# A routed two-pass expert kernel: how GpSimd's row gathers are spread over the pairs of tiles

## The chip, the cores and the metric

One core of one Trainium2 chip runs the kernel. The metric is the time of one execution in device microseconds; the time given is a median of several executions. A separate, profiled execution gives the trace.

## The reference, cut to what matters

```python
x = x + 0.5 * ffn(layernorm(x))        # pass 0
x = x + attention(layernorm(x))
x = x + 0.5 * ffn(layernorm(x))        # pass 1

def ffn(x):                            # x: 2048 tokens x 256
    scores = softmax(x @ gate_weight.T)            # 32 experts in 8 groups
    ... the best 3 groups, of those the best 6 experts for each token, weights normalised
    for e in range(32):                            # I = 128
        h = silu(x @ w1[e].T) * (x @ w3[e].T)
        y += combine[:, e, None] * (h @ w2[e].T)
    return y + silu(x @ sw1.T) * (x @ sw3.T) @ sw2.T      # the shared expert
```

Everything is float32. The attention between the two is a chunked linear attention over 16 heads; the change does not touch it.

## The kernel before, in words

The feed-forward part runs twice, as `moe(0)` and `moe(1)` (pass 0 and pass 1, `f` in the code). It does not compute every expert for every token. It sorts the 12288 choices (2048 tokens x 6) by expert, 96 full blocks of 128 rows, and cuts them into tiles of 128 rows that belong to one expert each. There are at most 128 such tiles, worked on in `NQ` = 64 pairs. The gathered rows make `NP` = 48 pairs of blocks; the last 16 pairs of tiles need no new rows.

The work of one pair q goes through the engines like this:

- GpSimd gathers the token rows of two blocks from a table in HBM by an indirect DMA (L399), into one of `RX` = 8 row buffers.
- TensorE transposes them two pairs ahead (`transpose_in`, L901, counts `e_xp`), VectorE copies them to a ring (L680, counts `e_in`), ScalarE picks the tile's columns (L492, `e_xt`).
- TensorE multiplies with w1 and w3 (`up`, L911, counts `e_h`), ScalarE takes the SiLU (`gate`, L469, `e_s`), VectorE multiplies (L690, `e_g`), TensorE transposes (L923), VectorE copies (L697), TensorE multiplies with w2 (`down`, L931), ScalarE copies the result out (`output`, L477, `e_y`), and SP stores two pairs at a time to a table of slots in HBM (L322), counting stored tiles in `s_there`.

ScalarE works in laps of `RA` = 4 pairs and reads register values for the ring columns at the start of each lap (L481). Every engine runs its instructions in the order written; engines meet only at semaphores.

When a column of results is there, its rows come back: GpSimd gathers, for the 16 blocks of tokens and for one of the six choices at a time ("column" n), the result rows from the table (L420), and VectorE adds them to x, weighted (`add_row`, L730). Pass 0 returns 2 columns this way (32 gathers, `returned` has 20 buffers), and leaves the other four columns to the attention part (L195). Pass 1 returns all six (96 gathers, `KEEP` = 28 buffers). Gather number g, counted over the columns, waits for `stored` (the tiles of that column are in the table), for a free buffer (`s_add`), and in pass 0 for `e_h`.

VectorE's last eight pairs (56 to 63) have four adds each: column 0 in pairs 56 to 59, column 1 in pairs 60 to 63 (L751 to L753). An add of a column waits until all 16 gathers of that column have landed (L721). These adds stand between the copy of one pair and the multiply of the next.

Behind pair 63 of pass 1, SP loads the tokens again (L353), TensorE computes the shared expert in four parts (L817, L830), and VectorE's order is fixed: adds of column 2, `product(0)` (L579), adds of column 3, `product(1)`, two shared additions (L669), adds of column 4, `product(2)`, shared additions, `product(3)`, adds of column 5 in two halves. TensorE's part n waits for `product(n - 1)`. In pass 0 the attention follows instead.

GpSimd's gathers of token rows wait on `e_xp`. With `AHEAD` = 4 and `EDGE` = 8, pass 0 lets pair q start once pair q - 4 has been transposed for q from 4 to 19, and once pair q - 8 has been from q = 20 on; pass 1 uses a lead of 4 for q from 4 to 11 and of 8 from q = 12 on.

Of the kernel before, what the change touches and what calls it, by code (L numbers as in the profile page):

```python
# [16 lines left out]
NT = T // P  # L17
# [11 lines left out]
NQ = ST // 2  # L29
# [7 lines left out]
RX = 8  # L37
EDGE = 8
AHEAD = 4
FILLS, FILL = 6, 8  # L40
EARLY = 2
REST = TOPK - EARLY
RY = 2
RA = 2 * RY
KEEP = 28
RO = 4
# [24 lines left out]
def begun(value):  # L71

    return not isinstance(value, int) or value > 0
# [7 lines left out]
def hold(eng, sem, value, held):  # L81

    eng.wait_ge(sem, value)
    eng.sem_inc(held, 1)
# [23 lines left out]
def program(nc, x_in, w13_in, w2_in, gate_in, sw13_in, sw2_in, wqkv_in, wg1_in, wg2_in, wo_in, nw_in,  # L110
            const_in, turn_in, out, table, y_table, columns_table):
    ctx = ExitStack()
    with ctx:
# [3 lines left out]
        def sem(name):  # L117
            return ctx.enter_context(nc.semaphore(name))
# [13 lines left out]
        def c(name, a=0, b=None):  # L132
# [5 lines left out]
        s_held, s_half, s_fill, s_again = sem("s_held"), sem("s_half"), sem("s_fill"), sem("s_again")  # L138
        s_rows, s_yst = [sem(f"s_rows{u}") for u in range(RX)], [sem(f"s_yst{u}") for u in range(RY)]
        e_xp, e_in, e_xt, e_h, e_s, e_g, e_gp, e_gt, e_yp, e_y = (  # L140
            sem(f"e_{n}") for n in ("xp", "in", "xt", "h", "s", "g", "gp", "gt", "yp", "y"))
# [21 lines left out]
        def inverse_root(chp, out, value, ready):  # L163

            chp(nc.gpsimd.tensor_tensor(out, value, eps_ln[:, :], ALU.add))
            nc.gpsimd.tensor_tensor(out, out, half[:, :], ALU.pow).then_inc(ready, 1)
# [37 lines left out]
        def moe(f, combine, share, ring, area, sw13, sw2):  # L204
# [7 lines left out]
            with ExitStack() as mem:  # L212
                def sb(name, shape, dt=F32):
                    return mem.enter_context(nc.sbuf_tensor(f"{name}_{f}", shape, dt))
# [24 lines left out]
                else:  # L239
                    y = [sb(f"ey{u}", [P, 4 * H]) for u in range(RY)]  # L240
                    s1, gTs = w13[:, 0:KS * TB], [w13[:, (u + 1) * KS * TB:(u + 2) * KS * TB] for u in range(2)]
# [39 lines left out]
                done, read = f * NQ, f * NP  # L281

                def v3(ap, k):
                    return ap.rearrange("p (t k) -> p t k", k=k)
# [11 lines left out]
                with nc.Block() as block:  # L296
                    @block.sync
                    def _(sp):
# [20 lines left out]
                        def store(it, u):  # L319
                            m = it * RY + u  # L320
                            sp.wait_ge(e_y, done + m * 2 + 2)
                            sp.dma_start(y_table.rearrange("(p t) h -> p t h", t=ST)[:, bass.ds(m * 4, 4), :],  # L322
                                         y[u].rearrange("p (t h) -> p t h", h=H)).then_inc(s_yst[u], 16)
                            if f == 1 or u > 0:
                                sp.wait_ge(s_yst[(u - 1) % RY], (it + f * (NQ // 2 // RY) + (u > 0)) * 16)
                            else:
                                sp.wait_ge(s_yst[(u - 1) % RY], it * 16)
                            sp.sem_inc(s_there, 4)  # L328
# [33 lines left out]
                    @block.gpsimd  # L362
                    def _(pool):
                        if f == 0:
                            nc.gpsimd.memset(half[:, :], -0.5).then_inc(s_half, 1)
                            chp(nc.gpsimd.memset(eps_ln[:, :], LN_EPS))

                        def sentinels():

                            for k in range(NG - TOPG):  # L370
                                value = -3.1e38 - 5e36 * k
                                nc.gpsimd.memset(low[:, k:k + 1], value)
                                last = nc.gpsimd.memset(v3(group, PADG)[:, :, NG + k:NG + k + 1], value)
                                if k < PADE - E:
                                    last = nc.gpsimd.memset(v3(val, PADE)[:, :, E + k:E + k + 1], value)
                            nc.gpsimd.memset(ones[:, :], 1.0)
                            nc.gpsimd.memset(most[:, :], 0.0)
                            nc.gpsimd.memset(ones16[:, :], 1.0).then_inc(s_low, 1)

                        if f == 0:  # L380
                            sentinels()
                        for k in range(NT // 2):
                            pool.wait_ge(s_var, 2 * k + 2)
                            inverse_root(chp, rs[:, 2 * k:2 * k + 2], v3(mv[:, :], 2)[:, 2 * k:2 * k + 2, 1], s_rstd)
                            if f == 1 and k == 1:
                                sentinels()

                        pool.wait_ge(s_st, 80)
                        pool.wait_ge(s_slots, 1)
                        for q in range(NP):  # L390
                            if f == 0 and AHEAD <= q < EDGE + RX + AHEAD:
                                pool.wait_ge(e_xp, q - AHEAD - max(0, q - EDGE - AHEAD) // EDGE + 1)
                            elif AHEAD <= q < EDGE + AHEAD:
                                pool.wait_ge(e_xp, read + q - AHEAD + 1)
                            elif q >= RX:
                                pool.wait_ge(e_xp, read + q - RX + 1)
                            for a in range(2):
                                t = 2 * q + a
                                pool.indirect_dma_start(  # L399
                                    out=rows[q % RX][:, a * H:(a + 1) * H], out_offset=None, in_=table,  # L400
                                    in_offset=bass.IndirectOffsetOnAxis(ap=slots[:, t:t + 1], axis=0)
                                ).then_inc(s_rows[q % RX], 16)

                        def stored(k):

                            end = pool.value_load(last_of_column[k:k + 1, 0:1], min_val=1, max_val=ST)
                            hold(pool, s_there, end + 4, s_held)

                        pool.wait_ge(s_known, 2)
                        pool.wait_ge(e_xp, read + NP)  # L410
                        for n in range(columns):
                            k = TOPK - 1 - n
                            stored(k)
                            for i in range(NT):
                                g = n * NT + i
                                if g >= len(returned):
                                    pool.wait_ge(s_add, g - len(returned) + 1)
                                if f == 0 and g % 2 == 0:
                                    pool.wait_ge(e_h, NQ - NT - 3 + g // 2)
                                pool.indirect_dma_start(  # L420
                                    out=returned[g % len(returned)], out_offset=None, in_=y_table,
                                    in_offset=bass.IndirectOffsetOnAxis(
                                        ap=combine[:, i * TOPK + k:i * TOPK + k + 1], axis=0)
                                ).then_inc(s_back[n] if n < TOPK - 1 else s_last[i // 4], 16)

                    @block.scalar
                    def _(act):
# [43 lines left out]
                        def output(q, u, lap):  # L471

                            act.wait_ge(e_yp, done + q + 1)
                            stored = (f * (NQ // RA) + lap) * 16
                            if u % 2 == 0 and begun(stored):
                                act.wait_ge(s_yst[u // 2], stored)
                            nc.scalar.copy(y[u // 2][:, u % 2 * 2 * H:(u % 2 + 1) * 2 * H], bY[u % 2][:, :]).then_inc(e_y, 1)  # L477
# [17 lines left out]

                        def pairs(q0, lap, n=RA, first=False, more=True):

                            column = columns_of(q0 * 2 + 2, 2 * n if more else 2 * n - 2)
                            for i in range(n):
                                if i < n - 1 or more:  # L500
                                    tile_columns(q0 + i + 1, i + 1, column[2 * i:2 * i + 2])
                                gate(q0 + i, i)
                                if i > 1 or not first:
                                    output(q0 + i - 2, (i - 2) % RA, lap - (i < 2))

                        act.wait_ge(s_known, 1)
                        tile_columns(0, 0, columns_of(0, 2))
                        pairs(0, 0, first=True)
                        with act.Fori(0, NQ // RA - 2) as it:
                            pairs(it * RA + RA, it + 1)  # L510
                        pairs(NQ - RA, NQ // RA - 1, more=False)
                        for u in range(2):
# [1190 lines left out]
```

## Time and profile before

| | |
|---|---|
| median of 3 executions | 966.11 us (962.2 to 973.23) |
| profiled execution | 960.5 us |
| its span, first to last instruction | 958.7 us |
| mean granted TensorE clock | 0.893 |
| GpSimd gathers of token rows (L399) | 192, mean 973 ns, 186.7 us busy |
| GpSimd gathers of returned rows (L420) | 124 + 4, mean 1049 ns |
| bytes moved by DMA | 126.43 MB, mean 132 GB/s |

In the rows of the next section, times are in microseconds from the start of the span unless marked ns. A line of the timeline gives start, duration, engine, source line, operation, what is written and read, how often, and in brackets how long the engine was idle before and what ended that. "x4" is four instructions merged. The trace names the source lines of the kernel above. Multiplies of VectorE (L690) can be counted: there are 64 in each pass, and multiply q is the one of pair q, counted from 0.

### The profile page before, as it was taken

To read this page: it belongs to the slowest core of one execution; us is meant where nothing else is said; L and a number is where in the kernel's file an instruction comes from. 1 tells how busy PE (TensorE), PEld (TensorE's weight loads), DVE (VectorE), ACT (ScalarE), POOL (GpSimd) and SP (SyncE) were. 2 spreads that over 40 slices of the span, in tenths; PEclk is the share of its full clock that TensorE was granted. 3 is DMA by queue.
4 is the path that set the end of the run, shared out by engine and by line. 5 is a ranking of instruction groups with operands and counts; after the bars stand their busy time and mean duration, and the time that the engine had idled before them with its cause. 6 is when DMAs were issued, how large, how long until landed. Compare 5 with 4: busy or idle time off the path is not lost. (4 is left out here: it accounts for less than half of the span.)

```text
span 958.7 us, 16120 instructions
## 1 busy us (share of the span) xinstructions
PE 772.8 (81%) x4554; PEld 609.0 (64%) x4555; DVE 513.0 (54%) x1439; ACT 358.5 (37%) x799; POOL 465.3 (49%) x487
## 2 busy tenths in 40 slices
PE   6895997999969789788889575686999995867486
PEld 6464885888847546576677374564888884645154
DVE  5774942434313537888887469672444431135274
ACT  3160443444424314465665224233444442322000
POOL 3005665553053335867754320655555406456884
PEclk9979898999988898999999755688999998887798
DMA  6862465643233463222220140233444413334524
GB/s 209 338 286 77 158 214 176 231 164 120 89 121 114 159 227 89 80 76 67 72 62 2 34 176 1 77 121 120 153 158 154 138 77 121 126 112 131 207 82 153
DMA packets 42358, 126.43 MB, mean 132 GB/s; under 512 B 8352, under 2 KB 16704, under 8 KB 39488
## 3 DMA queue, kind: packets, MB, share of 16 engines
q1 hardware_dynamic: 23872, 75.40, 20.7%
q0 software_dynamic: 18432, 50.36, 18.0%
q8 instruction: 29, 0.48, 0.2%
q14 instruction: 25, 0.20, 0.1%
HBM read 76.44 MB, written 49.28 MB: 131 GB/s over the span
## 5 line engine op out<-in xcount | busy, mean ns | idle before, releaser
L399 POOL DMA_INDIRECT back<-token_table,slots x192 | 186.7, 973 | 221.9 <-DVE slots L644 96.3
L911 PE MATMUL bank<-w,xt 128*128 x1024 | 260.7, 400 | 33.2 <-ACT xt L492 18.4
L911 PEld LDWEIGHTS bank<-w,xt 128*128 128x128 f32 x1024 | 196.5, 200 | 69.4 <-issue 44.2
L420 POOL DMA_INDIRECT back<-slot_table,combine x124 | 130.0, 1049 | 143.6 <-SPq L328 42.2
L690 DVE TENSOR_TENSOR mids<-mids,bank 128x256 f32<-128x256 f32 x128 | 53.8, 420 | 256.6 <-ACT mids L469 197.3
L931 PE MATMUL bank<-w,mids 128*128 x512 | 142.9, 405 | 4.5 <-DVE mids L697 2.6
L492 ACT COPY xt<-ring 128x256 f32 x256 | 91.5, 408 | 104.0 <-issue 75.9
L931 PEld LDWEIGHTS bank<-w,mids 128*128 128x128 f32 x512 | 93.2, 203 | 16.0 <-issue 7.1
L469 ACT ACTIVATE mids<-bank 128x256 f32<-128x256 f32 x128 | 49.0, 383 | 145.2 <-PE bank L911 87.8
L680 DVE COPY ring<-bank 128x512 f32 (+1 forms) x96 | 66.1, 689 | 46.6 <-PE bank L901 31.2
L923 PE MATMUL bank<-const,mids 128*128 128x128 f32 x256 | 52.6, 290 | 45.7 <-DVE mids L690 24.2
L195 POOL DMA_INDIRECT ring<-slot_table,combine x64 | 64.4, 1006 | 34.9 <-issue 17.4
L923 PEld LDWEIGHTS bank<-const,mids 128*128 128x128 f32 x256 | 36.7, 148 | 63.3 <-issue 29.4
L901 PE MATMUL bank<-const,back 128*128 128x128 f32 x384 | 60.9, 284 | 3.2 <-DMA back<-token_table,slots 3.2
L1111 POOL TENSOR_TENSOR root_a<-power_a,half 128x17 f32<-128x17 f32 (+2 forms) x20 | 51.3, 2564 | 21.1 <-DVE power_a L1465 13.0
L901 PEld LDWEIGHTS bank<-const,back 128*128 128x128 f32 x384 | 50.1, 147 | 14.3 <-DMA back<-token_table,slots 3.4
L477 ACT COPY ey<-bank 128x512 f32<-128x512 f32 x64 | 37.4, 584 | 54.7 <-PE bank L931 31.2
L697 DVE COPY mids<-bank 128x256 f32<-128x256 f32 x128 | 53.4, 417 | 5.7 <-PE bank L923 3.2
L477 ACT COPY gT<-bank 128x512 f32<-128x512 f32 x64 | 37.4, 585 | 49.9 <-PE bank L931 38.3
L730 DVE SCALAR_TENSOR_TENSOR x<-back,share,x 128x256 f32<-128x256 f32 x124 | 50.7, 477 | 4.1 <-DMA back<-slot_table,combine 3.9
L1483 DVE SCALAR_TENSOR_TENSOR ring<-bank,own_a 128x512 f32<-128x512 f32 x64 | 39.7, 683 | 14.4 <-remote 9.6
L817 PE MATMUL bank<-w,sw 128*128 128x512 f32 x64 | 32.0, 659 | 16.9 <-DMA w<-token_columns 12.3
(209 smaller groups left out, 1070.9 us busy)
## 6 DMA issues: line engine op xcount, KB each, us to landing
slot_table<-gT SPq DMA_DIRECT2D x32, 512.0 KB
slot_table<-ey SPq DMA_DIRECT2D x32, 512.0 KB
w<-in_w SPq DMA_DIRECT2D x12, 1024.0 KB, 17.1
slot_table<-w SPq DMA_DIRECT2D x6, 1024.0 KB
token_table<-back SPq DMA_DIRECT2D x8, 512.0 KB, 2.9
back<-token_table,slots POOLq DMA_INDIRECT x192
x<-in_x SPq DMA_DIRECT2D x4, 512.0 KB, 5.7
turn_a<-in_turn SPq DMA_DIRECT2D x4, 512.0 KB
```

The source lines that it names most:

```text
L195: nc.gpsimd.indirect_dma_start(out=back[j % RB][:, k * H:(k + 1) * H], out_offset=None, in_=y_table, in_offset=bass.IndirectOffsetOnAxis(a ...
L399: pool.indirect_dma_start(out=rows[q % RX][:, a * H:(a + 1) * H], out_offset=None, in_=table, in_offset=bass.IndirectOffsetOnAxis(ap=slots ...
L420: pool.indirect_dma_start(out=returned[g % len(returned)], out_offset=None, in_=y_table, in_offset=bass.IndirectOffsetOnAxis(ap=combine[:, ...
L477: nc.scalar.copy(y[u // 2][:, u % 2 * 2 * H:(u % 2 + 1) * 2 * H], bY[u % 2][:, :]).then_inc(e_y, 1)
L492: last = nc.scalar.copy(xt[u % 2][:, a * H:(a + 1) * H].rearrange("p (k i) -> p k i", k=KC), blocks[:, :, bass.ds(column[a], P)])
L680: last = nc.vector.tensor_copy(blocks[:, :, bass.ds(at, 2 * P)].rearrange("p k (a i) -> p k a i", a=2), new)
L690: nc.vector.tensor_tensor(two(eg[u % 2][:, :]), two(es[u % 2][:, :]), part(u, 1), ALU.mult).then_inc(e_g, 1)
L697: nc.vector.tensor_copy(egT[u % 2][:, :], bG[u % 2][:, 0:2 * P]).then_inc(e_gt, 1)
L901: last = nc.tensor.transpose(bX[u % 2][:, a * H + k * P:a * H + (k + 1) * P], rows[u][:, a * H + k * P:a * H + (k + 1) * P], ident)
L911: last = nc.tensor.matmul(bH[u % 2][:, a * 2 * I:(a + 1) * 2 * I], xt[u % 2][:, a * H + k * P:a * H + (k + 1) * P], w13[:, bass.ds(expert[ ...
L923: last = nc.tensor.transpose(bG[u % 2][:, a * P:(a + 1) * P], eg[u % 2][:, a * I:(a + 1) * I], ident)
L931: last = nc.tensor.matmul(bY[u % 2][:, a * H:(a + 1) * H], egT[u % 2][:, a * I:(a + 1) * I], w2[:, bass.ds(expert[a] * H, H)], start=True, ...
```

## The change

The wait ahead of the gathers of token rows becomes one rule for both passes: from pair 4 on, pair q waits until pair q - 4 of the same pass has been transposed. `read` is 0 in pass 0 and 48 in pass 1.

The wait ahead of the returned rows changes its numbers and now holds for both passes. With `done` 0 in pass 0 and 64 in pass 1, every second gather waits until `e_h` has reached 48 + g/2 in pass 0 (before: 45 + g/2), and 47 + g/2 in pass 1 (before: no such wait), as long as that number is at most 64. That is all 32 gathers in pass 0 and g up to 35 in pass 1. `e_h` counts finished up-products, so `e_h` = n means that up-product n - 1 is done. Nothing else is changed.

```diff
@@ constants
 RY = 2
+PACED = NQ - NT, NQ - NT - 1
 RA = 2 * RY
@@ GpSimd, gathers of token rows
                         for q in range(NP):
-                            if f == 0 and AHEAD <= q < EDGE + RX + AHEAD:
-                                pool.wait_ge(e_xp, q - AHEAD - max(0, q - EDGE - AHEAD) // EDGE + 1)
-                            elif AHEAD <= q < EDGE + AHEAD:
+                            if q >= AHEAD:
                                 pool.wait_ge(e_xp, read + q - AHEAD + 1)
-                            elif q >= RX:
-                                pool.wait_ge(e_xp, read + q - RX + 1)
                             for a in range(2):
@@ GpSimd, gathers of returned rows
                                 if g >= len(returned):
                                     pool.wait_ge(s_add, g - len(returned) + 1)
-                                if f == 0 and g % 2 == 0:
-                                    pool.wait_ge(e_h, NQ - NT - 3 + g // 2)
+                                if g % 2 == 0 and PACED[f] + g // 2 <= NQ:
+                                    pool.wait_ge(e_h, done + PACED[f] + g // 2)
                                 pool.indirect_dma_start(
```

## Rows read from the trace of the kernel before

**Rows 1.** The page, busy time, share of the span and instructions of each engine.
```profile
PE 772.8 (81%) x4554; PEld 609.0 (64%) x4555; DVE 513.0 (54%) x1439; ACT 358.5 (37%) x799; POOL 465.3 (49%) x487
```
**Rows 2.** Waits of ScalarE: who waited for whom, us in total, times, longest us.
```profile
ACT mids L469 <- remote: 54.8, 9, 8.7
...
ACT ey L477 <- remote: 14.9, 4, 8.1
...
ACT gT L477 <- remote: 6.7, 1, 6.7
```
**Rows 3.** The chain of work that ended last, around 650 us: start, us, what.
```profile
649.13 7.92 another core or an unknown queue
```
**Rows 4.** Timeline of VectorE, twelve multiplies of pairs 13 to 63, pass 0 then pass 1.
```profile
139.76 0.42 DVE L690 TENSOR_TENSOR mids<-mids,bank 128x256 f32<-128x256 f32 x1 [0.83 <-issue]
...
160.65 0.42 DVE L690 TENSOR_TENSOR mids<-mids,bank 128x256 f32<-128x256 f32 x1 [3.21 <-ACT mids L469]
...
176.73 0.42 DVE L690 TENSOR_TENSOR mids<-mids,bank 128x256 f32<-128x256 f32 x1 [0.82 <-issue]
...
188.22 0.42 DVE L690 TENSOR_TENSOR mids<-mids,bank 128x256 f32<-128x256 f32 x1 [2.98 <-ACT mids L469]
...
256.49 0.42 DVE L690 TENSOR_TENSOR mids<-mids,bank 128x256 f32<-128x256 f32 x1 [2.92 <-ACT mids L469]
...
264.29 0.42 DVE L690 TENSOR_TENSOR mids<-mids,bank 128x256 f32<-128x256 f32 x1 [2.06 <-ACT mids L469]
...
269.23 0.42 DVE L690 TENSOR_TENSOR mids<-mids,bank 128x256 f32<-128x256 f32 x1 [4.18 <-ACT mids L469]
...
334.24 0.42 DVE L690 TENSOR_TENSOR mids<-mids,bank 128x256 f32<-128x256 f32 x1 [0.47 <-ACT mids L469]
...
641.30 0.41 DVE L690 TENSOR_TENSOR mids<-mids,bank 128x256 f32<-128x256 f32 x1
...
662.70 0.42 DVE L690 TENSOR_TENSOR mids<-mids,bank 128x256 f32<-128x256 f32 x1 [3.79 <-issue]
...
793.70 0.42 DVE L690 TENSOR_TENSOR mids<-mids,bank 128x256 f32<-128x256 f32 x1 [2.06 <-ACT mids L469]
...
883.68 0.41 DVE L690 TENSOR_TENSOR mids<-mids,bank 128x256 f32<-128x256 f32 x1
```
**Rows 5.** Stretches: bounds, length, GpSimd busy (x instructions), clock, DMA share, GB/s.
```profile
137.00:152.00 15.00, 11.37 (x12) 0.93 0.63 211
176.00:191.00 15.00, 7.92 (x9) 1.00 0.61 216
267.00:284.50 17.50, 13.27 (x14) 0.86 0.48 147
...
637.50:656.00 18.50, 14.04 (x14) 0.97 0.42 131
```
**Rows 6.** Timeline of ScalarE, the copy out ahead of gate 15, pass 0.
```profile
154.24 0.59 ACT L477 COPY gT<-bank 128x512 f32<-128x512 f32 x1 [6.72 <-remote]
```
**Rows 7.** Timeline, the last gather of column 1 in pass 0 and its add.
```profile
324.03 1.19 POOL L420 DMA_INDIRECT back<-slot_table,combine  x1 [0.30 <-DVE x L730]
...
327.25 1.67 DVE L730 SCALAR_TENSOR_TENSOR x<-s,share,x 128x256 f32<-128x256 f32 x4 [1.67 <-DMA back<-slot_table,combine]
```
**Rows 8.** Stretches, line L420 alone; columns as in rows 5.
```profile
790.00:875.60 85.60, 47.77 (x50) 0.84 0.40 129
...
882.85:948.50 65.65, 52.47 (x44) 0.84 0.42 134
```
**Rows 9.** Timeline, the tail of pass 1: VectorE, gather 79, TensorE's weight load.
```profile
910.40 1.28 DVE L579 TENSOR_TENSOR w<-w,bank 128x512 f32<-128x512 f32 x2 [17.72 <-issue]
...
924.20 0.96 POOL L420 DMA_INDIRECT back<-slot_table,combine  x1 [0.30 <-issue]
...
927.03 6.42 DVE L730 SCALAR_TENSOR_TENSOR x<-back,share,x 128x256 f32<-128x256 f32 x16 [3.91 <-DMA back<-slot_table,combine]
...
934.70 0.40 PEld L817 LDWEIGHTS bank<-w,sw 128*128 128x128 f32 x2 [2.39 <-DVE w L579]
```

## The prediction

> **What bounds the kernel now.** I read the busy times first [rows 1]: TensorE is busy 81% of the span and GpSimd half of it, so the end is set by TensorE's pace and by what stops it. Then I read the waits [rows 2]. ScalarE waits for something the profile cannot name ("remote") 14 times in three groups, 76.4 us together, at most 8.7 us at once. The chain that ended last runs through such a wait [rows 3], so they are on the path: ScalarE hands the gate to VectorE, VectorE to TensorE, and all three stand.
>
> The pace is read from VectorE's multiply, one for each pair of tiles. Three pairs with the start of a ScalarE lap in them take 11.49 us (176.73 to 188.22) while TensorE also transposes gathered rows, and a whole lap of four takes 12.74 us (256.49 to 269.23) once it does not, 4.94 of it at the lap's start (264.29 to 269.23) and 7.8 in the other three pairs [rows 4].
>
> Last I asked what GpSimd does at the stalls [rows 5]. Where it issues gathers back to back (12 from 137 us, 14 from 267 us, 14 from 637.5 us), a ScalarE stall of 7 to 8 us falls inside or just behind. Where it issues two for each pair (9 in 15 us from 176 us), there is none, and the pace holds. The stalls also sit at different pairs of the two passes, though both run the same ScalarE loop: before pair 15 in pass 0 [rows 6], before pair 7 in pass 1 [rows 3]. I read this as: a row of eight or more gathers without a pause holds ScalarE up for about 7 us.
>
> **The change, part by part.**
>
> *Lead of four pairs throughout.* Before, pair 20 of pass 0 and pair 12 of pass 1 are where the wait falls back from four pairs to eight, and GpSimd issues four extra pairs at once. The change removes both bursts. Pass 0: multiply 13 to multiply 16 took 20.89 us (139.76 to 160.65), the same stretch of a later lap 11.49 [rows 4]: 9.4 us saved. Pass 1: multiply 5 to 8 took 21.40 us (641.30 to 662.70) against 11.49: 9.9 us saved. Cost: every gather now starts only four pairs ahead. Two take 2.2 to 2.5 us on GpSimd, and the last lands 2.0 us behind its end (325.22 to 327.25) [rows 7], against four pairs of lead, some 13 us; pass 0 already ran pairs 4 to 19 on it. I take nothing; if that cover went, TensorE's transposes would wait, and with 5 us of slack lost each lap this would be a large cost. The first bursts (75 us and 604 us) have the same waits as before and stay.
>
> *Returned rows, pass 0.* Before, gathers g and g+1 go once up-product 44 + g/2 is done (counted from 0), which let 14 leave in a row. Now it is up-product 47 + g/2. The first two start as before, since there the wait on the stores decides. Multiply 47 to 63 took 69.95 us (264.29 to 334.24). At the pace it is 4.94 + 3 x 12.74 + 7.8 = 51.0, so 19.0 go. A new wait comes: VectorE adds the second column's rows from pair 60 on and needs all 16. The last two now wait for up-product 62, which by the pace of 2.6 us ends about 4.8 us after multiply 60. Two gathers (2.2 to 2.5) and the landing (2.0) make 9.0 to 9.3, four adds (1.66) 10.7 to 11.0, where multiply 61 was due at 2.6. Queued behind the adds on VectorE are multiply 61 and the copy for TensorE, which stands meanwhile. About 1 us comes back, as up-product 62 is already done, and 1 goes to the lower clock that such pauses brought before. That is 8.1 to 8.4 us; I take 8.5, with bounds 0 (hidden) and 13. Net 10.5 saved.
>
> *Returned rows, pass 1.* Multiply 47 to 63 took 89.98 us (793.70 to 883.68), 39.0 above 51.0. The last two gathers of the second column wait for up-product 61, one pair earlier, so the same wait is 8.5 - 2.6 = 5.9; I take 5.5, bounds 0 and 10. Net 33.5 saved.
>
> *The tail of pass 1.* This is what the pacing costs. When up-product 63 ended (875.6 us), 50 of the 96 gathers had been issued [rows 8]; now it will be 34. The other 62 go back to back at 1.265 us each (0.96 and a gap of 0.30 [rows 9]). Let M be multiply 63. The gather that closes the fifth column (number 79) ended at M + 41.5 before (924.20 + 0.96). Now it ends at M - 0.2 + 46 x 1.265 = M + 58.0, or M + 64.6 if the slow gathers of the old tail recur (52.47 us busy for 44, where 44 x 0.96 is 42.2). VectorE already waited 3.91 us for that column, and product 2 and TensorE's last shared product follow it directly [rows 9]. So the lateness counts in full: +16.5 to +23, and +26 with the lower clock in TensorE's longer waits. I take +20. The columns before it are covered: the third lands by M + 20 to 24.5, and its 16 adds (6.4 us) are done about when product 0 is due (M + 26.7, 910.40). SP's stores and loads are not moved; the waits on stored rows are met before the new ones.
>
> Sum: -9.4 - 9.9 - 10.5 - 33.5 + 20 = -43.3 us. The profiled execution took 960.5 us (span 958.7), so it would take 917; the median of the runs shown lies 5.6 above it, and I predict **922 us** for the median.
>
> A rule that speaks against this: the Trainium skill (SBUF — State Buffer, Who interferes with whom) says that TensorE and ScalarE never wait on another engine at SBUF. By it no gather could hold ScalarE there and the sum would be rival A's. The rows show coincidence in every burst, not the path by which it acts; I go by the rows.
>
> **Rivals.**
>
> *A. The stalls belong to ScalarE's own stream, not to the gathers (slower).* The place is ScalarE's wait ahead of the gate and the output copy. For it: "remote" names no engine. Against: the different pairs in the two passes, and none in the steady stretch. Price: nothing saved, column waits 8.5 + 5.5, tail +20: 960.5 + 34 = 994, as a median 1000. It decides once less than 34 of the 77 us above the pace (9.4 + 9.9 + 19.0 + 39.0) go away. The Trainium skill (Runtime: NRT & Kernel Launch, Instruction fetch mechanics) has a mechanism for it: a taken branch to code outside the fetched pages stops an engine until a DMA has brought it. By that rule the time would be this rival's. No row here ties a stall to one.
>
> *B. Half the gain.* Two gathers for each pair, beside stores and adds, still provoke two or three stalls of 7.9 us between pairs 48 and 63: +16 to +24, so 938 to 946. For it: the old trace had most of its stalls there. Against: the pace holds with two for each pair elsewhere.
>
> *C. A wash.* The stalls get shorter instead of going: half of 77 saved, costs 34, so 956, as a median 961.
>
> *D. More.* The column waits are hidden and the tail stays at 16.5: 77.3 - 16.5 = 60.8 saved, 905 or less.
>
> **How the numbers follow.** The forecast has 0.62, with its own range 905 to 938 (column waits 0 to 13 and 0 to 10, tail 16.5 to 26). B has 0.17, A 0.09, C and D 0.06 each. The range 903 to 950 takes in the forecast, B and some of D. One per cent, 9.7 us, is about what a measurement of this kernel can tell from no change. Faster by more: forecast, B and D, 0.85. Same: C, 0.06. Slower: A, 0.09.
>
> **What would show it.** Right: no "remote" wait of ScalarE above 3 us around multiply 15 of pass 0 and multiply 7 of pass 1; returned gathers in twos about 3 us apart; VectorE waiting 5 us or more for a returned row at pair 60 of both passes; 34 returned gathers at up-product 63 of pass 1; the last shared product 65 to 75 us behind multiply 63, not 51. Wrong: ScalarE stalls of 7 us with gathers in twos (A or B), or an end later than 101 us behind multiply 63 (75.0 before).

## The result and the profile after

The changed kernel took 926.6 us (median of 4, 919.38 to 927.35) against 964.91 us (median of 4, 962.2 to 973.23). The ratio is 0.957, 95% interval 0.950 to 0.965: faster by 4.3%. The profiled execution took 926.16 us, 34.3 us less than the 960.5 us before.

The changed code is three lines shorter, so L466 is now ScalarE's gate, L474 its output copy, L687 the multiply, L727 the add of returned rows, L417 the gather of returned rows, L576 and L814 the product and TensorE's shared products. The waits first (who waited for whom, us in total, times, longest us):

```profile
DVE x L727 <- DMA back<-slot_table,combine: 64.0, 5, 17.0
...
ACT mids L466 <- remote: 11.7, 3, 7.5
```

ScalarE's "remote" waits are down from 14 with 76.4 us [rows 2] to 3 with 11.7 us at the gate, and one more of 2.1 us in the attention (L1334); the one of 7.5 us is that of the very first row of gathers, which the change leaves alone. VectorE now waits 64.0 us for returned rows.

**Who is late in a "remote" wait.** The profile writes "remote" where a semaphore rises and no instruction that raises it ended in the 1.5 us before. It does not mean that nobody is known to raise it. Here is the stall of pair 7 of pass 1 in the kernel before: the up-product of TensorE, the gate of ScalarE that waits for it, TensorE's next matmuls, and the gather of GpSimd that waits for TensorE's transposes:

```profile
649.37 1.99 PE L911 MATMUL bank<-w,xt 128*128 x8 [1.67 <-issue]
...
657.08 0.38 ACT L469 ACTIVATE mids<-bank 128x256 f32<-128x256 f32 x1 [7.95 <-remote]
...
658.04 0.69 PE L923 MATMUL bank<-const,mids 128*128 128x128 f32 x2 [6.69 <-DVE mids L690]
...
658.15 0.96 POOL L399 DMA_INDIRECT back<-token_table,slots  x1 [2.38 <-remote]
```

The up-product ends at 651.36 in the profile, where the ends of matmuls are modelled. Its count `e_h` rises at 657.05 in the trace's semaphore records, 5.7 us later, and the gate starts at once. All 31 "remote" waits of this trace, 14 of ScalarE, 10 of VectorE and 7 of GpSimd, are waits for a count that TensorE raises, and so are the 223 in the nine other traces below that have any. The results of ScalarE and VectorE came on time: in the 128 pairs of this trace the multiply, the transposes and the down-product start at most 0.15 us after what they wait for and their own engine are ready, while the gate starts up to 8.2 us after. So ScalarE is not what is held: TensorE's results, or its word of them, come late, and whoever needs them waits. Whether the matmuls themselves ran long or only their counts were late is not shown. "ScalarE stalls" in the texts below is to be read in this way.

What GpSimd does in the stretches that had rows of 12 and 14 gathers (bounds, length, busy and instructions, clock, DMA share, GB/s):

```profile
137.00:152.00 15.00, 8.44 (x9) 1.00 0.61 220
176.00:191.00 15.00, 8.51 (x9) 1.00 0.50 173
```

The stretch from 137 us has the same nine gathers as the quiet one, and TensorE's granted clock is 1.00 in it; before it was 12 gathers at 0.93 [rows 5]. The multiplies of pairs 16, 47 and 63 of pass 0, then 5, 47 and 63 of pass 1, answer to [rows 4]:

```profile
151.25 0.42 DVE L687 TENSOR_TENSOR mids<-mids,bank 128x256 f32<-128x256 f32 x1 [2.78 <-ACT mids L466]
...
254.84 0.42 DVE L687 TENSOR_TENSOR mids<-mids,bank 128x256 f32<-128x256 f32 x1 [2.06 <-ACT mids L466]
...
318.14 0.42 DVE L687 TENSOR_TENSOR mids<-mids,bank 128x256 f32<-128x256 f32 x1 [1.70 <-ACT mids L466]
...
627.41 0.41 DVE L687 TENSOR_TENSOR mids<-mids,bank 128x256 f32<-128x256 f32 x1
...
769.02 0.42 DVE L687 TENSOR_TENSOR mids<-mids,bank 128x256 f32<-128x256 f32 x1 [2.06 <-ACT mids L466]
...
826.92 0.42 DVE L687 TENSOR_TENSOR mids<-mids,bank 128x256 f32<-128x256 f32 x1 [1.50 <-ACT mids L466]
```

Multiply 47 to 63 takes 63.3 us in pass 0 (69.95 before) and 57.9 us in pass 1 (89.98 before). The waits that took the stalls' place are the adds of column 1 at pair 60 (one line for each pass) and, in the tail, those of columns 3 and 4, the last followed by TensorE's last shared product:

```profile
310.28 1.67 DVE L727 SCALAR_TENSOR_TENSOR x<-s,share,x 128x256 f32<-128x256 f32 x4 [12.06 <-DMA back<-slot_table,combine]
...
819.21 0.92 DVE L727 SCALAR_TENSOR_TENSOR x<-back,share,x 128x256 f32<-128x256 f32 x2 [7.31 <-DMA back<-slot_table,combine]
...
869.54 6.42 DVE L727 SCALAR_TENSOR_TENSOR x<-back,share,x 128x256 f32<-128x256 f32 x16 [13.47 <-DMA back<-slot_table,combine]
...
892.56 6.42 DVE L727 SCALAR_TENSOR_TENSOR x<-back,share,x 128x256 f32<-128x256 f32 x16 [14.21 <-DMA back<-slot_table,combine]
...
900.23 0.50 PEld L814 LDWEIGHTS bank<-w,sw 128*128 128x128 f32 x2 [11.37 <-DVE w L576]
```

The gathers of returned rows of pass 1, ahead of the last multiply and behind it (L417 alone), answer to [rows 8]:

```profile
760.00:826.50 66.50, 32.84 (x34) 0.95 0.42 138
826.50:924.00 97.50, 67.89 (x62) 0.79 0.43 138
```

34 before and 62 behind, as counted ahead of time. Behind the last pair GpSimd issues almost without a pause. TensorE waits for products there, and its granted clock is 0.79 on average, against 0.84 in the tail before [rows 8].

### The profile page after: what moved, and what is told of

It is laid out like the page before. It is cut to its first block and busy times, and to the rows that moved or that the text cites. A ratio compares the mean times of both kernels' runs of the same rounds, so it can differ in the third digit from the quotient of the medians.

```text
span 924.4 us, 16124 instructions
## 1 busy us (share of the span) xinstructions
PE 761.2 (82%) x4554; PEld 602.4 (65%) x4555; DVE 512.7 (55%) x1439; ACT 359.2 (39%) x799; POOL 462.8 (50%) x487
## 3 DMA queue, kind: packets, MB, share of 16 engines
q1 hardware_dynamic: 23872, 75.40, 21.4%
## 5 line engine op out<-in xcount | busy, mean ns | idle before, releaser
L908 PE MATMUL bank<-w,xt 128*128 x1024 | 251.7, 390 | 16.5 <-ACT xt L489 12.3
L908 PEld LDWEIGHTS bank<-w,xt 128*128 128x128 f32 x1024 | 191.0, 195 | 49.0 <-issue 25.9
L417 POOL DMA_INDIRECT back<-slot_table,combine x124 | 127.9, 1031 | 101.8 <-PE bank L908 64.0
L687 DVE TENSOR_TENSOR mids<-mids,bank 128x256 f32<-128x256 f32 x128 | 53.7, 420 | 193.1 <-ACT mids L466 143.3
L928 PE MATMUL bank<-w,mids 128*128 x512 | 135.5, 388 | 1.6 <-DVE mids L694 1.6
L928 PEld LDWEIGHTS bank<-w,mids 128*128 128x128 f32 x512 | 88.9, 194 | 10.6 <-issue 3.2
L466 ACT ACTIVATE mids<-bank 128x256 f32<-128x256 f32 x128 | 48.8, 381 | 93.5 <-PE bank L908 76.9
L727 DVE SCALAR_TENSOR_TENSOR x<-back,share,x 128x256 f32<-128x256 f32 x124 | 50.8, 479 | 52.1 <-DMA back<-slot_table,combine 52.0
L920 PE MATMUL bank<-const,mids 128*128 128x128 f32 x256 | 50.3, 279 | 23.9 <-DVE mids L687 23.8
L814 PE MATMUL bank<-w,sw 128*128 128x512 f32 x64 | 36.5, 734 | 35.0 <-DVE w L576 22.3
L898 PE MATMUL bank<-const,back 128*128 128x128 f32 x384 | 60.4, 282 | 3.3 <-DMA back<-token_table,slots 3.2
L474 ACT COPY ey<-bank 128x512 f32<-128x512 f32 x64 | 37.3, 583 | 38.2 <-PE bank L928 32.6
L474 ACT COPY gT<-bank 128x512 f32<-128x512 f32 x64 | 37.3, 583 | 37.7 <-PE bank L928 32.7
L814 PEld LDWEIGHTS bank<-w,sw 128*128 128x128 f32 x64 | 14.9, 241 | 55.3 <-issue 34.8
```

What stands on the lines that cost most here:

```text
L417: pool.indirect_dma_start(out=returned[g % len(returned)], out_offset=None, in_=y_table, in_offset=bass.IndirectOffsetOnAxis(ap=combine[:, ...
L727: nc.vector.scalar_tensor_tensor(x[:, i * H:(i + 1) * H], returned[g % len(returned)], share[:, i * TOPK + k:i * TOPK + k + 1], x[:, i * H ...
L814: last = nc.tensor.matmul(bS[m][:, :], sw13[:, k * 2 * SI + m * P:k * 2 * SI + (m + 1) * P], tokens[:, k * T + its[it] * TB:k * T + (its[i ...
L898: last = nc.tensor.transpose(bX[u % 2][:, a * H + k * P:a * H + (k + 1) * P], rows[u][:, a * H + k * P:a * H + (k + 1) * P], ident)
L908: last = nc.tensor.matmul(bH[u % 2][:, a * 2 * I:(a + 1) * 2 * I], xt[u % 2][:, a * H + k * P:a * H + (k + 1) * P], w13[:, bass.ds(expert[ ...
L920: last = nc.tensor.transpose(bG[u % 2][:, a * P:(a + 1) * P], eg[u % 2][:, a * I:(a + 1) * I], ident)
```

## The experiments

The kernels ran in four groups; the kernels of a group and the kernel before shared one chip. The groups fell on four chips (that of the result above is not on record), and this turned out to matter: the kernel before took 885.5 us on chip 5, 964.0 us on chip 2, 968.0 us on chip 9 and 967.3 us on chip 0.

### Each half of the change alone, and the rhythm of the gathers (chip 5)

`lead_only` is the kernel before with the new wait ahead of the token rows; `paced_only` is the changed kernel with the old one, that is the diff below read backwards:

```diff
-                            if f == 0 and AHEAD <= q < EDGE + RX + AHEAD:
-                                ...
+                            if q >= AHEAD:
                                 pool.wait_ge(e_xp, read + q - AHEAD + 1)
```

> The kernel before with the fixed lead of four pairs alone; the returned rows as before. If rows of gathers hold ScalarE up: the two stalls at multiply 15 of pass 0 and multiply 7 of pass 1 go (9.4 + 9.9 us), those behind multiply 47 stay: about 945 us, ratio 0.98. If the stalls belong to ScalarE's own stream (rival A), they come back at the same multiplies or nearby: 960 to 970 us.

Measured: 884.8 us (10 executions) against 885.5 us (13); ratio 1.000, interval 0.998 to 1.001.

> The changed kernel with the old lead of the token rows; only the returned rows are paced. If rows of gathers are the cause: stalls of 7 us at multiply 15 of pass 0 and 7 of pass 1, none behind multiply 47 of either pass, tail of pass 1 about 97 us: 945 to 955 us. Rival A: stalls behind multiply 47 stay and the new waits come on top, 990 us or more.

Measured: 902.2 us; ratio 1.020, interval 1.017 to 1.022.

`group4` and `group8` keep every gather of the changed kernel and change only when the token rows leave, from pair 16 on of each pass (n = 2 or 4 pairs together):

```diff
-                            if q >= AHEAD:
-                                pool.wait_ge(e_xp, read + q - AHEAD + 1)
+                            if AHEAD <= q < 2 * RX:
+                                pool.wait_ge(e_xp, read + q - AHEAD + 1)
+                            elif q >= 2 * RX and (q - 2 * RX) % n == 0:
+                                pool.wait_ge(e_xp, read + min(q + n, NP) - RX)
```

> The changed kernel, but from pair 16 on of each pass the token rows of two pairs leave together: 4 gathers in a row every two pairs, the same number in all. If a row must have eight or more gathers to hold ScalarE up: no stall, 920 to 930 us. If any row longer than two does: stalls at most of 32 places, over 1000 us. If the gathers' rhythm has no part (rival A): unchanged, 920 to 930 us.

Measured: 906.3 us, one execution.

> The changed kernel, but from pair 16 on of each pass the token rows of four pairs leave together: 8 gathers in a row every four pairs, 8 rows of 8. If rows of eight hold ScalarE up for about 7 us, and TensorE loses 5 of them: eight stalls, 965 us or more. If the row must be longer than eight, or rival A holds: unchanged, 920 to 930 us.

Measured: 900.6 us, one execution.

All four expectations missed, because each took the stalls or the times of the first trace for granted on any chip. On this one nothing stalls. The trace of `lead_only` has no "remote" wait of any engine, although it issues its returned rows as the kernel before does. Two stretches of pass 1 with 20 gathers each, columns as above:

```profile
744.00:768.00 24.00, 18.21 (x20) 1.00 0.60 191
768.00:793.00 25.00, 19.07 (x20) 1.00 0.57 185
```

and its multiplies 47 and 63 of pass 1:

```profile
742.28 0.42 DVE L686 TENSOR_TENSOR mids<-mids,bank 128x256 f32<-128x256 f32 x1 [2.06 <-ACT mids L465]
...
792.33 0.42 DVE L686 TENSOR_TENSOR mids<-mids,bank 128x256 f32<-128x256 f32 x1 [0.44 <-ACT mids L465]
```

50.05 us, where the prediction worked out 51.0 for "without stalls". So the pace was right, and this chip shows the change's costs alone. From multiply 63 of pass 1 on, `lead_only` takes 88.9 us (792.33 to the end of the span, 881.2) and `paced_only` 97.8; ahead of it `paced_only` takes 58.5 us from multiply 47 instead of 50.05. That is 17.4 us, the difference of the medians, and all but 2.3 us of that of the two spans (900.9 and 881.2). In pass 0 there is almost none: 60.4 and 60.7 us, since with 20 buffers the old order waits at pair 60 too (10.2 us in `lead_only`, 10.7 us in `paced_only`).

### The same two kernels again, and a better place for the adds (chip 2)

> The kernel before, unchanged, for its trace. If rows of gathers hold ScalarE up on every chip: the stalls of 7 to 8 us as in the first trace, 960 us. If the stalls are a property of where it ran (the two runs before this one showed none, with the old lead or the old pacing): no wait of ScalarE called remote above 1 us, about 885 us, and 51 us from multiply 47 to 63 of pass 1.

Measured: 976.64 us, one execution, in a group whose 7 executions of the same kernel have a median of 964.0 and a highest of 969.4. The stalls are there. ScalarE's "remote" waits (us in total, times, longest us):

```profile
ACT mids L469 <- remote: 59.2, 10, 9.8
...
ACT w L445 <- remote: 27.2, 2, 14.6
...
ACT ey L477 <- remote: 23.6, 3, 10.2
...
ACT gT L477 <- remote: 7.9, 2, 5.3
```

The two waits of L445 lie in the tail of pass 1, where ScalarE waits for TensorE's shared products beside gathers in a row, and VectorE has one of 7.0 us there (L669). This tail took 89.2 us instead of the 75.0 of the first trace, so stalls are not confined to the loop over the pairs.

> The changed kernel, unchanged. Where the kernel before shows the stalls: ratio 0.95 to 0.97. Where it shows none: the costs of the pacing stand alone, the wait at pair 60 of pass 1 (7 us) and the later tail (9 us), 902 us against 885, ratio 1.02.

Measured: 921.7 us (4); ratio 0.954, interval 0.949 to 0.960. The result repeats.

`late_adds` moves the 16 adds of column 1 behind the last pair (the first diff); `late_free` does that and also takes the pacing out of pass 1 (the second):

```diff
-                                    for g in range(i * 2 * NT // n, (i + 1) * 2 * NT // n):
-                                        add_row(g // NT, g % NT)
+                                    for g in range(i * 2 * NT // n, min((i + 1) * 2 * NT // n, NT)):
+                                        add_row(0, g)
...
                         copy_mid(NQ - 1, NQ - 1)
+                        for i in range(NT):
+                            add_row(1, i)
```

```diff
-                                if g % 2 == 0 and PACED[f] + g // 2 <= NQ:
+                                if f == 0 and g % 2 == 0 and PACED[f] + g // 2 <= NQ:
```

> The changed kernel with the 16 adds of column 1 moved behind the last pair, in both passes. Theory: VectorE's wait at pair 60 (10 us above the pace in pass 0, 7 in pass 1) goes, and the adds fit into idle time of VectorE behind the loop: 14 to 18 us less than the changed kernel, about 886 where there are no stalls. Rival: the adds of pass 0 delay the attention by as much as they freed (6.6 us), and the tail of pass 1, bound by GpSimd, takes back its 7: no more than 5 us gained.

Measured: 905.8 us (4); ratio 0.9385, interval 0.933 to 0.944: 15.9 us less than the changed kernel, and the best of all on this chip. Its waits for returned rows:

```profile
DVE x L727 <- DMA back<-slot_table,combine: 40.3, 4, 14.2
```

23.5 us and one wait less than in the changed kernel on this chip (63.8, 5). Multiply 47 to 63 takes 51.0 us in pass 0 and 50.2 us in pass 1, where `after_again` takes 62.4 and 57.5: both are now at the pace. Of these 18.7 us some come back: multiply 63 of pass 0 to multiply 5 of pass 1 takes 308.6 us instead of 305.8, and behind multiply 63 of pass 1 it takes 99.8 us instead of 97.5. That is 5.1 us, so the rival (the adds only move the delay) falls.

> As the one with late adds, and pass 1 returns its rows without pacing. Where there are no stalls: pass 0 gains 10 us on the kernel before, pass 1 is as before, about 875 us. Where rows of gathers stall ScalarE: behind multiply 47 of pass 1 four or five stalls come back, 30 us above the one with late adds ahead of the tail.

Measured: 930.2 us (4); ratio 0.965, interval 0.960 to 0.970. The stalls behind multiply 47 of pass 1 are back, two of them in the timeline of ScalarE (its line numbers are those of the changed kernel):

```profile
770.67 0.58 ACT L474 COPY ey<-bank 128x512 f32<-128x512 f32 x1 [8.75 <-remote]
...
820.50 0.58 ACT L474 COPY ey<-bank 128x512 f32<-128x512 f32 x1 [5.52 <-remote]
```

So on a chip that stalls, pacing pass 1 is worth 24.4 us net of its later tail.

### Rows of eight where there had been twos (chip 9)

> The changed kernel with the token rows of four pairs leaving together from pair 16 on, 8 gathers in a row. On a chip like the one with stalls: if a row of eight (10 us) is enough, some of the eight rows stall ScalarE by 5 to 8 us, 20 us or more above the changed kernel's 922 (or its ratio of 0.955 to the kernel before is lost to 0.98 or more); if not, ratio 0.955. On a chip like the one without: 900 us against 885 as measured there.

Measured: 998.1 us (2); ratio 1.032, interval 1.024 to 1.040. It is the same file that took 900.6 us on chip 5. The lap of four pairs in which a row of eight falls has stalls, all sixteen times. Here are the stretch with one row of eight and, from the timeline of ScalarE, the stalls of two laps:

```profile
175.00:190.00 15.00, 7.55 (x8) 0.87 0.52 175
```

```profile
184.37 0.38 ACT L468 ACTIVATE mids<-bank 128x256 f32<-128x256 f32 x1 [4.92 <-PE bank L910]
...
187.36 0.59 ACT L476 COPY gT<-bank 128x512 f32<-128x512 f32 x1 [2.60 <-remote]
...
203.68 0.38 ACT L468 ACTIVATE mids<-bank 128x256 f32<-128x256 f32 x1 [4.82 <-PE bank L910]
...
206.64 0.59 ACT L476 COPY gT<-bank 128x512 f32<-128x512 f32 x1 [2.58 <-remote]
```

The gate's waits of 4.9 and 4.8 us are of the same kind; the up-product that the first waits for ended at 180.4, its count rose at 184.35, and the profile names TensorE because its next up-product had just ended. Such a lap takes 16.7 to 19.9 us, and about 13.7 in the changed kernel. With the gathers' number, sizes and addresses unchanged, when they leave is enough to make the stalls. The clock averages 0.87 in that stretch, and 1.00 in the same one of the changed kernel. The edit also lets rows leave up to eight pairs ahead instead of four; the kernel before has that lead too, with gathers in twos and no stall, in its steady laps of 13.7 us.

> The version with late adds again. On a chip with stalls: 0.94 of the kernel before. On one without: it takes back the 7 us of pass 1 and 10 us of pass 0 that the wait at pair 60 costs, but not the tail: 885 to 890 us against 885, ratio 1.00 to 1.01.

Measured: 910.8 us (4); ratio 0.941, interval 0.936 to 0.946. The gain of the late adds repeats on a third chip.

### How long a row may be (chip 0)

> The changed kernel with 4 gathers in a row every two pairs from pair 16 on. On a chip with stalls: rows of four come some 1.5 us apart here, so either they are short enough (no stall, 922 to 930 us, ratio 0.955 to 0.965), or the hold-up grows with the row and costs 1 us or more at each of 32 rows: 950 us or more, ratio 0.98 or more. On a chip without: 906 us as measured.

Measured: 946.5 us (2); ratio 0.980, interval 0.973 to 0.987. Neither expectation describes this, though 0.980 is the second one's edge. The rows of four do show: VectorE's ring copies wait for TensorE's transposes as in the line below, once in most laps. But a lap takes 13.9 us instead of 13.7, some 1 us in each pass.

```profile
191.52 0.69 DVE L679 COPY ring<-bank 128x512 f32 x1 [2.75 <-remote]
```

The loss sits at the one place per pass where the lead grows from four pairs, and ten gathers leave in a row: multiply 9 to 16 takes 32.5 us in pass 0 (25.1 in the changed kernel) and 33.4 us in pass 1 (25.2). The kernel before had just such a place at pair 20 and at pair 12. These two places and the longer laps make some 18 us; against the changed kernel's 921.7 us, taken on another chip, 25 are to be explained, and where the rest lies is not shown.

> The kernel before with the fixed lead alone. On a chip with stalls: the stalls at multiply 15 of pass 0 and 7 of pass 1 go, 9.5 and 10.8 us, the others stay: ratio 0.98. If the stalls only move to the next place: ratio 1.00. On a chip without: ratio 1.00 as measured.

Measured: 949.3 us (5); ratio 0.983, interval 0.978 to 0.989. As expected: multiply 13 to 16 of pass 0 takes 11.4 us, 5 to 8 of pass 1 10.5 us, and the stalls behind multiply 47 stay.

## Why the prediction was right

It was right in the time (926.6 against 922), in the sign, and in what makes the stalls: rows of gathers without a pause. It was wrong in whom they hold: not ScalarE, but TensorE's results or its word of them (see the section on the result). The sum did not need the name of the engine, as it was made from the stretches that the stalls had lengthened. Some of the closeness is luck: for the profiled execution it forecast 917 us, and it took 926.2, 9 us of the saving missed. The 5.6 us that were added to get from there to the median hid half of that, for the median after lies only 0.4 us above the profiled execution. Each term can be read off (profiled executions; multiplies as marks; saved is positive):

| stretch | predicted | measured |
|---|---|---|
| pass 0, multiply 13 to 16 | 9.4 | 20.9 - 11.4 = 9.5 |
| pass 0, multiply 47 to 63 | 10.5 | 69.95 - 63.3 = 6.7 |
| pass 0 multiply 63 to pass 1 multiply 5 (attention) | 0 | 307.1 - 309.3 = -2.2 |
| pass 1, multiply 5 to 8 | 9.9 | 21.4 - 10.6 = 10.8 |
| pass 1, multiply 47 to 63 | 33.5 | 90.0 - 57.9 = 32.1 |
| behind multiply 63 of pass 1 | -20 | 75.0 - 97.5 = -22.5 |
| sum | 43.3 | 34.4 |

The attention row is within what runs of one file differ by: the same stretch took 309.3 us here and 305.8 us in `after_again`.

*The lead of four pairs.* The cost of nothing held: over multiplies 16 to 47 of pass 0 both kernels take 103.6 us, with a lead of eight pairs before and of four after.

*The wait at pair 60* was mis-sized, in pass 0: multiply 61 followed multiply 60 after 14.4 us, not 10.7 to 11.0. Two things were missed. GpSimd itself waited 1.6 us for TensorE's count ahead of the last four gathers, which then left in one row; and the last landed 3.6 us after its end (306.7 to 310.3), not 2.0. In pass 1 it took 9.7 us; 8.1 to 8.4 had been the sum before the clock. The stall-free laps of pass 0 were also not quite free: multiply 50 came after 4.8 us and 59 after 3.9, with ScalarE waits of 1.8 and 2.5 us, where gathers had merged into rows of four to six.

*The tail.* Column 4's adds began at M + 65.6 (892.56), inside the 60.0 to 66.6 that the gathers' count gives with the landing, at its late end, because the slow gathers recurred (67.89 us busy for 62). All of it counted in full, as said: from 854 us to the landing ahead of column 4's adds at 892 us, the chain of work that ended last is almost nothing but one gather after another.

*Rival A* (the stalls belong to ScalarE's own stream) falls with `group8_b`: eight gathers in a row, put where twos had been, bring new stalls there, and taking rows away takes the stalls away, in both passes (`lead_only_b`) and in one (`late_free` against `late_adds`). The waits for TensorE speak against it too. Nor does loading of code show: the two queues of kind "instruction" moved 54 packets in the trace of the kernel before, and the same 54 in that of `lead_only`, which has no stall. *B, C and D* did not come.

*What the prediction did not see* is that all of this depends on the chip. It read one trace and took the stalls as a property of the kernel. On chip 5 the same rows of gathers cost nothing; there `lead_only` is at 1.000 and `paced_only` at 1.020, so both halves together would make the kernel slower there by about 2% (worked out from the halves: the changed kernel itself did not run on that chip, nor did the late adds). `group4` and `group8`, which have both halves, took 906.3 and 900.6 us there.

*A rival that no run tests* is the recording. Every execution timed in the four groups has its span and its granted clock on record, so each was recorded. The traces with stalls have lost part of their semaphore records, and the four of chip 5 have not: of VectorE's 128 copies at L697, 88 counts are left in the kernel before, and `lead_only` has all. The issues of token-row gathers show it as well, first the kernel before, then `lead_only`; the last figure, the time to landing, is given only where the records of all landings are there:

```profile
back<-token_table,slots POOLq DMA_INDIRECT x192
```

```profile
back<-token_table,slots POOLq DMA_INDIRECT x192, 2.8
```

So where the stalls are, the recording also went differently. Whether it has a part in them, or both have one cause, is open, and with it what the change is worth in an execution that nobody records.

The objection from the Trainium skill (SBUF — State Buffer, Who interferes with whom) is not refuted. ScalarE does wait in rows of gathers, 7.95 us at 683.85 us of `group8_b`, but for TensorE's count and not, as far as any trace shows, at SBUF. What holds TensorE or its counts no run shows. A kernel that spaces the gathers with other GpSimd work, with no wait on TensorE, was not tried.

## What to carry to other kernels

At each wait that the profile does not name, look up which engine raises that semaphore, and what GpSimd does at that time: on three of the four chips of these experiments, TensorE's results came up to 10 us late (`lead_only_b`) beside indirect DMAs issued eight or more in a row, and in time or nearly so beside two for each step of the loop. Pacing has a price at the end of the stream, so move consumers that need the last row (here 16 adds) behind the loop, where their engine is idle. And measure such a change on more than one chip before it is called a gain.

## What the runs showed of the hardware

The same kernel took 885.5 us on chip 5 and 964 to 968 us on chips 2, 9 and 0, with a spread of 5 us on the first and 7 to 11 on the others. The trace of `lead_only` on chip 5 has no "remote" wait at all, while the kernel before has 31 elsewhere, ScalarE's alone 76.4 us [rows 2]. TensorE's mean granted clock there was 0.916 (`lead_only`, span 881.2 us) against 0.893 before.

In the ten traces with such waits, all 254 are for counts that TensorE raises. The stalls sit beside rows of gathers in the loop over the pairs, and in one trace in the tail as well (`before_again`: 12.6 and 14.6 us of ScalarE). Why some chips do this is open.
